# A mixture-of-experts stage whose first weights are half doubled by ScalarE and asked for at another point

## The chip, the cores and the metric

The kernel runs on one core of a Trainium2 chip. The metric is the device time of one execution in microseconds; lower is better. TensorE is called PE here, VectorE DVE, ScalarE ACT, GpSimd POOL and SyncE SP, as in the profile. SP does no arithmetic in this kernel, it waits for semaphores and issues DMA transfers.

## What is computed

The reference is a two-layer language-model tower over 64 x 128 tokens of width 192. In short:

```python
h = layernorm(tok_w[x] + pos_w + type_w[mask]) * gamma + beta
h = h + attention(layernorm(h))                       # layer 0
h = h + moe(layernorm(h))                             # the stage of this case
h = h + attention_with_relative_positions(layernorm(h))   # layer 1
h = h + fast_feed_forward(layernorm(h))

def moe(xf):                     # E = 8 experts, top K = 2, D = 192, I = 768
    gates = softmax(xf @ Wr + br)
    top_g, top_i = top_k(gates, 2)
    for e in range(8):
        w_e = sum(top_g * (top_i == e), axis=-1)
        y = gelu(xf @ W1[e] + b1[e], exact) @ W2[e] + b2[e]
        out = out + w_e[:, None] * y
```

## The kernel before

The kernel is one program in stages: layer 0 (64 token tiles in a software pipeline), the routing (which token goes to which seat of which expert), the expert stage, layer 1 and a short last stage. Only the expert stage is touched.

**Tiles of the expert stage.** The 16,384 pairs of token and expert are sorted by expert into 71 tiles (NBLK) of 256 rows (BLK), each tile with one expert. For each tile the kernel loads that expert's weights anew, gathers the tile's 256 token rows from `zn_d`, computes the 768 hidden values (transposed, in 6 chunks of 128, kept in `prob`, in the code `hT`), and the 192 outputs, and stores them to `ys_d`. All buffers of the stage are double: tile t uses number t mod 2.

**The product in parts.** Each fp32 weight w is split into a high part of the type float32r and a low part w - high, and so is x. DVE makes `w1hi` (L1152, two casts of 768 columns, one for rows 0 to 127 of the weights and one for rows 128 to 191) and `w1lo` (L1154, L1155, two subtractions). The weights have 192 rows; the second piece of them, 64 rows, was loaded twice, to partitions 0 to 63 and 64 to 127 of `w1[b][1]`. The rows gathered from `zn_d` hold the last 64 columns twice as well, so that on the second piece the upper 64 partitions of `xhi` can hold the low part of x (L1160): one product covers high and low. PE runs 5 products for each of 6 chunks (L1024 to L1030).

**The engines' programs**, all built by `pipeline` (L107), which calls a body for each step n and tells it by an age which tile each part works on: `load` has age 0, `h` age 1, `y` age 2.

- SP (`expert_sync`, L1172): at step n waits until all GELUs of tile n-2 are done (`h_sb`, L1194), issues the four loads of first weights and bias of tile n (L1199), waits until the outputs of tile n-2 are added (`y_sb`, L1201), issues second weights and their bias (L1203, L1205), and then stores the outputs of tile n-2 (L1210). It also issues, at step 2, the store of the routing table, at step 5 its reload (L1183), and at steps 4 to 7 four reads of `hres` for layer 1 (L1188), one a step, ahead of that step's loads.
- POOL (`expert_pool`, L947): gathers the rows of a tile (L964) when the tile of two before has been transposed.
- PE (`expert_tensor`, L983): transposes of tile t (L993, L994), second product of tile t-1 (L1005, called y here), waits for `xhi`, `xlo` and `split` of tile t, first product of tile t (L1030, called h).
- ACT (`expert_scalar`, L1050): copies the transposed x out of PSUM (`xhi`, L1055), then six GELUs (L1061), two behind each pair of chunks.
- DVE (`expert_vector`, L1144): waits for the first weights (L1150), splits them, makes `xlo` (L1158) and the low rows (L1160), and adds the output bias of tile t-1 (L1168, `ys`).

The first weights lie in the tile `score` by the profile's names, the second ones in `probT`, the output bias in `tok`.

Of the kernel before, what the change touches and what calls it, by code (L numbers as in the profile page):

```python
# [7 lines left out]
F32 = mybir.dt.float32  # L8
# [4 lines left out]
ACT = mybir.ActivationFunctionType  # L13
# [4 lines left out]
D1 = D - 128  # L18
# [5 lines left out]
E, TOPK, I = 8, 2, 768  # L24
NI = I // 128
BLK = 256
NBLK = T * B * TOPK // BLK + E - 1
# [42 lines left out]
def upto(t, tiles=NT):  # L70

    return max(0, min(t + 1, tiles)) if isinstance(t, int) else t + 1


def after(eng, sem, value):

    if not isinstance(value, int) or value > 0:
        eng.wait_ge(sem, value)
# [58 lines left out]
def settle(eng, spare):  # L137

    eng.sem_inc(spare, 1)


def tower(nc, ids_h, typ_h, tok_w, pos_w, type_w, gamma, beta,
# [7 lines left out]
    with ExitStack() as ctx:  # L150
# [6 lines left out]
        def sem(name):  # L157
            return ctx.enter_context(nc.semaphore(name))
# [64 lines left out]
        idx = two("idx", [128, 1], U32)  # L223
# [40 lines left out]
        b1s = two("b1s", [128, NI])  # L264
# [39 lines left out]
        spare = sem("spare")  # L304
# [598 lines left out]
                                         "tables", "lane", "seat", "seat_mm", "seated", "rows")}  # L903
        route_st, route_ld = sem("route_st"), sem("route_ld")
        h1_ld = [sem(f"h1_ld{c}") for c in range(4)]
        D_ = {n: sem("D_" + n) for n in ("xT_ps", "xhi_sb", "xlo_sb", "split", "dve", "idx", "h_ps", "h_sb", "y_ps", "y_sb")}
        w1_ld = [sem(f"w1_ld{p}") for p in range(2)]
        x_ld = [sem(f"x_ld{p}") for p in range(2)]
        w2_ld = [sem(f"w2_ld{p}") for p in range(2)]
        y_st = [sem(f"y_st{p}") for p in range(2)]  # L910
        ages_d = dict(load=0, h=1, y=2)
        NH = NI // 2
        ps_y = [ps_v, ps_k]

# [67 lines left out]

        def expert_tensor(pe):  # L983
            def body(st):
                t = st.n - 1
                if st.has("h"):
                    b = st.two("h")
                    pe.wait_ge(x_ld[b], 32 * (st.pair("h") + 1))

                    after(pe, D_["xhi_sb"], upto(t - 1, NBLK))  # L990
                    after(pe, D_["xlo_sb"], upto(t - 1, NBLK))
                    for s in range(2):
                        pe.transpose(ps_t[:, s * 128:s * 128 + 128], xs[b][:, s, 0:128], ident[:])  # L993
                        last = pe.transpose(ps_t[:, BLK + s * 128:BLK + s * 128 + 128], xs[b][:, s, 128:XW],  # L994
                                            ident[:])
                    last.then_inc(D_["xT_ps"], 1)
                if st.has("y"):
                    b = st.two("y")
                    pe.wait_ge(w2_ld[b], 32 * (st.pair("y") + 1))
                    after(pe, D_["y_sb"], upto(t - 2, NBLK))  # L1000
                    for j in range(NH):
                        pe.wait_ge(D_["h_sb"], NH * st.tile("y") + j + 1)
                        for c in (2 * j, 2 * j + 1):
                            for s in range(2):
                                last = pe.matmul(ps_y[s][:, 0:D], hT[b][:, c, s * 128:s * 128 + 128],  # L1005
                                                 w2[b][:, c, :], start=(c == 0), stop=(c == NI - 1))
                    last.then_inc(D_["y_ps"], 1)
                if st.has("h"):
                    b = st.two("h")
                    pe.wait_ge(D_["xhi_sb"], upto(t, NBLK))  # L1010
                    pe.wait_ge(D_["xlo_sb"], upto(t, NBLK))
                    pe.wait_ge(D_["split"], upto(t, NBLK))
                    for j in range(NH):

                        if not (isinstance(t, int) and t == 0):
                            pe.wait_ge(D_["h_sb"], NH * (t - 1) + j + 1)
                        for c in (2 * j, 2 * j + 1):
                            dst = ps_s[:, j, (c % 2) * BLK:(c % 2) * BLK + BLK]
                            u = slice(c * 128, c * 128 + 128)

                            terms = [(w1hi[b][0][:, u], xhi[b][:, 0:BLK]),  # L1024
                                     (w1lo[b][0][:, u], xhi[b][:, 0:BLK]),
                                     (w1hi[b][0][:, u], xlo[b][:]),
                                     (w1hi[b][1][:, u], xhi[b][:, BLK:2 * BLK]),
                                     (w1lo[b][1][:, u], xhi[b][:, BLK:2 * BLK])]
                            for k, (w, x) in enumerate(terms):
                                last = pe.matmul(dst, w, x, start=(k == 0), stop=(k == len(terms) - 1))  # L1030
                        last.then_inc(D_["h_ps"], 1)
            pipeline(pe, ages_d, body, tiles=NBLK)
# [17 lines left out]
        def expert_scalar(act):  # L1050
            def body(st):
                if st.has("h"):
                    t, b = st.tile("h"), st.two("h")
                    act.wait_ge(D_["xT_ps"], upto(t, NBLK))
                    act.activation(xhi[b][:], ps_t[:], ACT.Copy).then_inc(D_["xhi_sb"], 1)  # L1055
                    for j in range(NH):
                        act.wait_ge(D_["h_ps"], NH * t + j + 1)

                        after(act, D_["y_ps"], upto(t - 2, NBLK))
                        for c in (2 * j, 2 * j + 1):  # L1060
                            last = act.activation(hT[b][:, c, :], ps_s[:, j, (c % 2) * BLK:(c % 2) * BLK + BLK],  # L1061
                                                  ACT.Gelu, bias=b1s[b][:, c:c + 1])
                        last.then_inc(D_["h_sb"], 1)
            pipeline(act, ages_d, body, tiles=NBLK)
# [78 lines left out]

        def expert_vector(dve):  # L1144
            ch = Chain(dve, D_["dve"])

            def body(st):
                if st.has("h"):
                    t, b = st.tile("h"), st.two("h")
                    dve.wait_ge(w1_ld[b], 64 * (st.pair("h") + 1))  # L1150
                    for c in range(2):
                        ch.step(dve.tensor_copy(w1hi[b][c][:], w1[b][c]))  # L1152
                    ch.done()
                    dve.tensor_tensor(w1lo[b][0][:], w1[b][0], w1hi[b][0][:].bitcast(F32), ALU.subtract)  # L1154
                    dve.tensor_tensor(w1lo[b][1][:], w1[b][1], w1hi[b][1][:].bitcast(F32),  # L1155
                                      ALU.subtract).then_inc(D_["split"], 1)
                    dve.wait_ge(D_["xhi_sb"], upto(t, NBLK))
                    dve.tensor_tensor(xlo[b][:], ps_t[:, 0:BLK], xhi[b][:, 0:BLK].bitcast(F32), ALU.subtract)  # L1158
                    rest = xhi[b][D1:128, BLK:2 * BLK]
                    dve.tensor_tensor(rest, ps_t[D1:128, BLK:2 * BLK], rest.bitcast(F32), ALU.subtract)\  # L1160
                        .then_inc(D_["xlo_sb"], 1)
                if st.has("y"):
                    t, b = st.tile("y"), st.two("y")
                    dve.wait_ge(D_["y_ps"], upto(t, NBLK))

                    after(dve, y_st[b], 16 * st.pair("y"))
                    for s in range(2):
                        ins = dve.tensor_tensor(ys[b][:, s, :], ps_y[s][:, 0:D], b2s[b], ALU.add)  # L1168
                    ins.then_inc(D_["y_sb"], 1)
            pipeline(dve, ages_d, body, ch, 2, tiles=NBLK)  # L1170

        def expert_sync(sp):  # L1172
# [1 line left out]
            hv = h1_d.rearrange("(t b) d -> b t d", b=B)  # L1174

            def body(st):
                before2 = upto(st.n - 2, NBLK)
                if isinstance(st.n, int) and st.n == 2:
                    sp.wait_ge(B_["turned"], 1)
                    sp.dma_start(route_d.rearrange("q (n k) -> n q k", n=NT), turned[:]).then_inc(route_st, 16)  # L1180
# [9 lines left out]
                if st.has("load"):  # L1190
                    t, b = st.tile("load"), st.two("load")
                    ex = sp.value_load(etabi[0:1, bass.ds(t, 1)], min_val=0, max_val=E - 1)

                    after(sp, D_["h_sb"], NH * before2)  # L1194
                    settle(sp, spare)
                    loads = [(w1[b][0], w1h[bass.ds(ex, 1), 0:128, :]), (b1s[b][:], b1h[bass.ds(ex, 1)])]
                    loads += [(w1[b][1][r:r + D1, :], w1h[bass.ds(ex, 1), 128:, :]) for r in (0, D1)]
                    for dst, src in loads:
                        sp.dma_start(dst, src.rearrange("o k i -> (o k) i")).then_inc(w1_ld[b], 16)  # L1199

                    after(sp, D_["y_sb"], before2)  # L1201
                    settle(sp, spare)
                    sp.dma_start(probT[b][:, 0:NI * D], w2h[bass.ds(ex, 1), :, :].rearrange("o k i -> (o k) i"))\  # L1203
                        .then_inc(w2_ld[b], 16)
                    sp.dma_start(b2s[b], b2h[bass.ds(ex, 1), :].to_broadcast([128, D])).then_inc(w2_ld[b], 16)  # L1205
# [413 lines left out]
```

## Time and profile before

| | us |
|---|---|
| median of 3 runs | 1827.81 |
| lowest, highest | 1826.41, 1836.93 |
| the profiled execution | 1831.29 |
| its span, first to last instruction | 1829.6 |
| mean granted clock of TensorE over the span | 0.970 |

| engine | busy us | share of the span |
|---|---|---|
| PE | 1645.3 | 90% |
| DVE | 1314.9 | 72% |
| ACT | 1172.6 | 64% |
| POOL | 659.8 | 36% |

The times are from separate executions, the profile from one. Its page lists busy time per engine over the whole span, which is a mean over stages with different limits. The timeline lists instructions by start with their length, and in square brackets how long the engine sat idle before and what ended that. Names stand as output<-inputs, with buffer numbers left out. `SPq` is SP's queue of DMA issues: a length there is the time that the issue took, not the transfer.

### The profile page before, as it was taken

To read this page: it belongs to the slowest core of one execution; us is meant where nothing else is said; L and a number is where in the kernel's file an instruction comes from. 1 tells how busy PE (TensorE), PEld (TensorE's weight loads), DVE (VectorE), ACT (ScalarE), POOL (GpSimd) and SP (SyncE) were. 2 spreads that over 40 slices of the span, in tenths; PEclk is the share of its full clock that TensorE was granted. 3 is DMA by queue.
4 is the path that set the end of the run, shared out by engine and by line. 5 is a ranking of instruction groups with operands and counts; after the bars stand their busy time and mean duration, and the time that the engine had idled before them with its cause. 6 is when DMAs were issued, how large, how long until landed. Compare 5 with 4: busy or idle time off the path is not lost. (4 is left out here: it accounts for less than half of the span.)

```text
span 1829.6 us, 60456 instructions
## 1 busy us (share of the span) xinstructions
PE 1645.3 (90%) x19438; PEld 1502.9 (82%) x19438; DVE 1314.9 (72%) x2962; ACT 1172.6 (64%) x3337; POOL 659.8 (36%) x1326
## 2 busy tenths in 40 slices
PE   2999999999578799999999999579999999999966
PEld 2888888888367699999999999468888888888852
DVE  5888888887585255555555554289999999999855
ACT  2888888888374233333333333389999999999930
POOL 4455555553103133333333332334444444444200
PEclk9999999999788899999999999899999999999978
DMA  4122222222124978888888888377777777777614
GB/s 114 45 65 61 65 61 62 63 61 53 35 65 116 296 231 242 246 243 247 243 246 240 246 244 226 93 217 206 207 208 217 207 214 213 208 209 212 195 41 138
DMA packets 349282, 301.77 MB, mean 165 GB/s; under 512 B 43915, under 2 KB 314335, under 8 KB 349215
## 3 DMA queue, kind: packets, MB, share of 16 engines
q1 hardware_dynamic: 328878, 261.16, 49.6%
q0 software_dynamic: 16032, 37.51, 8.5%
q10 hardware_dynamic: 4304, 2.23, 0.5%
q8 instruction: 39, 0.64, 0.1%
q14 instruction: 29, 0.23, 0.0%
HBM read 207.77 MB, written 93.05 MB: 164 GB/s over the span
## 5 line engine op out<-in xcount | busy, mean ns | idle before, releaser
L1061 ACT ACTIVATE prob<-ps_s,b1s 128x256 f32<-128x256 f32 x426 | 179.2, 472 | 371.3 <-PE ps_s L1030 371.3
L1030 PE MATMUL ps_s<-xhi,w1hi_c 128*128 128x256 f32 x852 | 237.9, 297 | 19.8 <-DVE xhi L1160 18.1
L1030 PE MATMUL ps_s<-xhi,w1lo_c 128*128 128x256 f32 x852 | 228.5, 286 | 0.0
L964 POOL DMA_INDIRECT xs<-zn_d,idx x71 | 93.9, 1323 | 356.5 <-PE ps_t L994 354.0
L1152 DVE CAST w1hi_c<-score 128x768 fp32r<-128x768 f32 x142 | 73.3, 558 | 205.1 <-DMA score<-w1h 204.9
L1005 PE MATMUL ps_v<-probT,prob 128*128 128x192 f32 x852 | 208.3, 326 | 0.0
L1005 PE MATMUL ps_k<-probT,prob 128*128 128x192 f32 x852 | 208.1, 326 | 0.0
L396 PE MATMUL ps_q<-xT,wqk_c 128*128 128x128 f32 x1536 | 196.8, 279 | 1.1 <-ACT kT L643 0.6
L396 PEld LDWEIGHTS ps_q<-xT,wqk_c 128*128 128x128 f32 x1536 | 189.5, 196 | 1.9 <-ACT xT L664 1.0
L1030 PEld LDWEIGHTS ps_s<-xhi,w1hi_c 128*128 128x128 f32 x852 | 165.7, 195 | 22.4 <-issue 20.3
L1030 PEld LDWEIGHTS ps_s<-xhi,w1lo_c 128*128 128x128 f32 x852 | 165.8, 195 | 0.0
L583 ACT ACTIVATE prob<-score 128x768 f32<-128x768 f32 (+1 forms) x128 | 149.2, 1166 | 3.1
L1005 PEld LDWEIGHTS ps_k<-probT,prob 128*128 128x128 f32 x852 | 150.2, 190 | 0.0
L1005 PEld LDWEIGHTS ps_v<-probT,prob 128*128 128x128 f32 x852 | 146.6, 190 | 0.0
L735 DVE TENSOR_TENSOR score<-ps_s,relb 128x1536 f32<-128x1536 f32 x64 | 112.4, 1756 | 31.8 <-DMA relb<-rel_d 25.1
L456 PEld LDWEIGHTS ps_v<-vv,probT 128*64 128x64 f32 x3072 | 102.4, 139 | 30.6 <-issue 28.3
L1030 PE MATMUL ps_s<-xlo,w1hi_c 128*128 128x256 f32 x426 | 121.6, 285 | 0.0
L382 PE MATMUL ps_s<-kT,qT 32*64 32x64 f32 (+1 forms) x4608 | 113.4, 253 | 5.2 <-ACT xT L664 4.9
L456 PE MATMUL ps_v<-vv,probT 128*64 128x17 f32 x3072 | 113.3, 212 | 5.2 <-DVE hres L778 3.5
L382 PEld LDWEIGHTS ps_s<-kT,qT 32*64 32x64 f32 (+1 forms) x4608 | 91.9, 151 | 27.7 <-issue 27.5
L435 PE MATMUL ps_k<-ident,prob 128*128 128x128 f32 x704 | 112.8, 279 | 1.6 <-ACT prob L583 1.6
L321 POOL TENSOR_TENSOR rs<-veps,mhalf 128x1 f32<-128x1 f32 x192 | 108.1, 563 | 15.0
(217 smaller groups left out, 4385.1 us busy)
## 6 DMA issues: line engine op xcount, KB each, us to landing
rel_d<-rpad SPq DMA_DIRECT2D x64, 864.0 KB
relb<-rel_d SPq DMA_DIRECT2D x64, 768.0 KB, 4.7
probT<-w2h SPq DMA_DIRECT2D x71, 576.0 KB
score<-w1h SPq DMA_DIRECT2D x71, 384.0 KB
score<-w1h SPq DMA_DIRECT2D x142, 192.0 KB
ys_d<-ys SPq DMA_DIRECT2D x71, 192.0 KB
tok<-b2h SPq DMA_DIRECT2D x71, 96.0 KB
posb<-pos_w SPq DMA_DIRECT2D x128, 48.0 KB
```

The source lines that it names most:

```text
L321: pool.tensor_tensor(out[b][:], veps[b][:], mhalf[:, 0:1], ALU.pow).then_inc(S[out_ok], 1)
L382: last = pe.matmul(ps_s[t, g, a * keys:a * keys + keys], qT[q4][q, a // 2, t], kT[q4][q, a, t], start=True, stop=True)
L396: last = pe.matmul(ps_q[:, o:o + 128], qk_w[l][chunk][:, o:o + 128], (xT0, xT1)[chunk][b][:], start=(chunk == 0), stop=(chunk == 1))
L435: last = pe.transpose(ps_pt[u % 2][:, k * 128:k * 128 + 128], prob[b][:, j * 128:j * 128 + 128], ident[:])
L456: last = pe.matmul(ps_v[64 * c:64 * c + 64, j * W:(j + 1) * W], probT[b][:, j * 128 + 64 * c:j * 128 + 64 * c + 64], vv[v][:, j * W:(j + 1 ...
L583: act.activation(prob[b][:, 0:H * keys].rearrange("p (g a k) -> p g a k", g=G, a=A), score[b][:, :, :, 0:keys], ACT.Exp, scale=SCALE).then ...
L735: dve.tensor_tensor(sc, psv, relb[b][:].rearrange("p (g a) k -> p g a k", g=G), ALU.add).then_inc(S["s_rd"], 1)
L964: pool.indirect_dma_start(xs[b][:, s, :], None, zn_d, bass.IndirectOffsetOnAxis(ap=ix[b][:], axis=0)).then_inc(x_ld[b], 16)
L1005: last = pe.matmul(ps_y[s][:, 0:D], hT[b][:, c, s * 128:s * 128 + 128], w2[b][:, c, :], start=(c == 0), stop=(c == NI - 1))
L1030: last = pe.matmul(dst, w, x, start=(k == 0), stop=(k == len(terms) - 1))
L1061: last = act.activation(hT[b][:, c, :], ps_s[:, j, (c % 2) * BLK:(c % 2) * BLK + BLK], ACT.Gelu, bias=b1s[b][:, c:c + 1])
L1152: ch.step(dve.tensor_copy(w1hi[b][c][:], w1[b][c]))
```

## The change

- SP issues one load of the second piece of the first weights (to partitions 0 to 63) where it issued two.
- DVE casts and subtracts only partitions 0 to 63 of the second piece. The upper rows of `w1lo[.][1]` are cleared once, ahead of the stage. Low part of w times low part of x on these rows, a term of second order, is thereby left out, as it is on the first piece.
- ACT copies partitions 0 to 63 of the loaded second piece to partitions 64 to 127 of `w1hi[.][1]` for each tile, between `xhi` and the GELUs, and counts `twice`. PE waits for `twice` as well ahead of the first product.
- The ages are now `w1` 0, `load` 1, `h` 2, `y` 3. At step n SP works in this order: wait for `h_sb` of tile n-3, load b1 of tile n-1; wait for `split` and `twice` of tile n-2, load first weights of tile n; wait for `y_sb` of tile n-3, load second weights and bias of tile n-1; store tile n-3. The step numbers of the routing table and of the `hres` reads are as they were.
- b1 has a semaphore of its own, and ACT waits for it ahead of the GELUs.

```diff
-        ages_d = dict(load=0, h=1, y=2)
+        b1_ld = [sem(f"b1_ld{p}") for p in range(2)]
+        ages_d = dict(w1=0, load=1, h=2, y=3)
...
                     pe.wait_ge(D_["split"], upto(t, NBLK))
+                    pe.wait_ge(D_["twice"], upto(t, NBLK))
...
                     act.activation(xhi[b][:], ps_t[:], ACT.Copy).then_inc(D_["xhi_sb"], 1)
+                    act.wait_ge(w1_ld[b], 32 * (st.pair("h") + 1))
+                    act.activation(w1hi[b][1][D1:128, :], w1[b][1][0:D1, :], ACT.Copy).then_inc(D_["twice"], 1)
+                    act.wait_ge(b1_ld[b], 16 * (st.pair("h") + 1))
...
             ch = Chain(dve, D_["dve"])
+            for p in range(2):
+                ch.step(dve.memset(w1lo[p][1][D1:128, :].bitcast(F32), 0.0))
+            ch.done()
...
-                    dve.wait_ge(w1_ld[b], 64 * (st.pair("h") + 1))
-                    for c in range(2):
-                        ch.step(dve.tensor_copy(w1hi[b][c][:], w1[b][c]))
+                    dve.wait_ge(w1_ld[b], 32 * (st.pair("h") + 1))
+                    ch.step(dve.tensor_copy(w1hi[b][0][:], w1[b][0]))
+                    ch.step(dve.tensor_copy(w1hi[b][1][0:D1, :], w1[b][1][0:D1, :]))
...
-                    dve.tensor_tensor(w1lo[b][1][:], w1[b][1], w1hi[b][1][:].bitcast(F32),
+                    low = w1lo[b][1][0:D1, :]
+                    dve.tensor_tensor(low, w1[b][1][0:D1, :], w1hi[b][1][0:D1, :].bitcast(F32),
                                       ALU.subtract).then_inc(D_["split"], 1)
...
-                    after(sp, D_["h_sb"], NH * before2)
+                    after(sp, D_["h_sb"], NH * upto(t - 2, NBLK))
                     settle(sp, spare)
-                    loads = [(w1[b][0], w1h[bass.ds(ex, 1), 0:128, :]), (b1s[b][:], b1h[bass.ds(ex, 1)])]
-                    loads += [(w1[b][1][r:r + D1, :], w1h[bass.ds(ex, 1), 128:, :]) for r in (0, D1)]
+                    sp.dma_start(b1s[b][:], b1h[bass.ds(ex, 1)].rearrange("o k i -> (o k) i")).then_inc(b1_ld[b], 16)
+                if st.has("w1"):
+                    t, b = st.tile("w1"), st.two("w1")
+                    ew = sp.value_load(etabi[0:1, bass.ds(t, 1)], min_val=0, max_val=E - 1)
+
+                    after(sp, D_["split"], upto(t - 2, NBLK))
+                    settle(sp, spare)
+
+                    after(sp, D_["twice"], upto(t - 2, NBLK))
+                    settle(sp, spare)
+                    loads = [(w1[b][0], w1h[bass.ds(ew, 1), 0:128, :])]
+                    loads += [(w1[b][1][0:D1, :], w1h[bass.ds(ew, 1), 128:, :])]
                     for dst, src in loads:
                         sp.dma_start(dst, src.rearrange("o k i -> (o k) i")).then_inc(w1_ld[b], 16)
-
-                    after(sp, D_["y_sb"], before2)
+                if st.has("load"):
+                    t, b = st.tile("load"), st.two("load")
+
+                    after(sp, D_["y_sb"], upto(t - 2, NBLK))
```

## Rows read from the trace of the kernel before

**Rows 1.** PE row of the page's 40 slices, 45.7 us each, busy tenths.

```profile
PE   2999999999578799999999999579999999999966
```

**Rows 2.** Windows: length, PE, PEld, DVE, ACT, POOL busy, PEclk, DMA share, GB/s.

```profile
575.00:595.68 20.68, 20.68 (x151) 20.68 (x150) 9.96 (x20) 6.65 (x16) 7.81 (x12) 1.00 0.81 230
595.68:646.54 50.86, 35.92 (x235) 34.86 (x234) 17.13 (x32) 12.03 (x28) 11.71 (x16) 0.90 0.99 283
700.00:800.00 100.00, 100.00 (x736) 100.00 (x734) 52.04 (x100) 37.81 (x88) 33.35 (x51) 1.00 0.87 246
```

**Rows 3.** Timeline of ACT: start, length, line and operation, idle time before.

```profile
595.68 0.84 ACT L1061 ACTIVATE prob<-ps_s,b1s 128x256 f32<-128x256 f32 x2 [4.20 <-PE ps_s L1030]
...
646.54 0.84 ACT L1061 ACTIVATE prob<-ps_s,b1s 128x256 f32<-128x256 f32 x2 [6.37 <-PE ps_s L1030]
...
853.40 0.84 ACT L1061 ACTIVATE prob<-ps_s,b1s 128x256 f32<-128x256 f32 x2 [4.20 <-PE ps_s L1030]
...
861.33 0.84 ACT L1061 ACTIVATE prob<-ps_s,b1s 128x256 f32<-128x256 f32 x2 [4.20 <-PE ps_s L1030]
```

**Rows 4.** Timeline of ACT near the end of the expert stage.

```profile
1115.38 0.84 ACT L1061 ACTIVATE prob<-ps_s,b1s 128x256 f32<-128x256 f32 x2 [4.20 <-PE ps_s L1030]
...
1142.17 0.84 ACT L1061 ACTIVATE prob<-ps_s,b1s 128x256 f32<-128x256 f32 x2 [5.88 <-PE ps_s L1030]
```

**Rows 5.** Timeline of DVE between 600 and 645 us.

```profile
606.28 1.03 DVE L1152 CAST w1hi_c<-score 128x768 fp32r<-128x768 f32 x2 [11.16 <-DMA score<-w1h]
...
641.24 1.03 DVE L1152 CAST w1hi_c<-score 128x768 fp32r<-128x768 f32 x2 [7.20 <-DMA score<-w1h]
```

**Rows 6.** Timeline of one steady tile, SP's queue, DVE, PE and ACT.

```profile
850.02 1.15 SPq L1199 DMA_DIRECT2D score<-w1h  x2
...
853.09 0.34 SPq L1203 DMA_DIRECT2D probT<-w2h  x1
...
855.22 1.03 DVE L1152 CAST w1hi_c<-score 128x768 fp32r<-128x768 f32 x2 [2.29 <-DMA score<-w1h]
...
855.60 0.27 PE L993 MATMUL ps_t<-ident,xs 128*128 128x128 f32 x1
...
856.04 0.49 PE L1005 MATMUL ps_v<-probT,prob 128*128 128x192 f32 x2
...
856.53 0.60 ACT L1055 ACTIVATE xhi<-ps_t 128x512 fp32r<-128x512 f32 x1
...
858.46 0.43 DVE L1160 TENSOR_TENSOR xhi<-ps_t,xhi 64x256 fp32r<-64x256 f32 x1
...
859.80 0.42 PE L1030 MATMUL ps_s<-xhi,w1hi_c 128*128 128x256 f32 x1
```

**Rows 7.** Timeline of SP's queue from 580 to 598 us.

```profile
580.40 0.42 SPq L1210 DMA_DIRECT2D ys_d<-ys  x1
...
588.79 0.46 SPq L1188 DMA_DIRECT2D hres<-h_d  x1
...
591.23 4.36 SPq L1199 DMA_DIRECT2D score<-w1h  x1
...
596.31 1.12 SPq L1199 DMA_DIRECT2D score<-w1h  x2
```

**Rows 8.** DMA issues of the page: KB each.

```profile
probT<-w2h SPq DMA_DIRECT2D x71, 576.0 KB
score<-w1h SPq DMA_DIRECT2D x71, 384.0 KB
score<-w1h SPq DMA_DIRECT2D x142, 192.0 KB
```

**Rows 9.** Lines by form, ACT: count, busy us, mean ns, idle before.

```profile
L576 ACT ACTIVATE probT<-ps_q 128x512 f32<-128x512 f32 x64 | 38.3, 598 | 5.0 <-PE ps_q L435 5.0
...
L576 ACT ACTIVATE probT<-ps_q 128x384 f32<-128x384 f32 x64 | 31.9, 498 | 0.0
```

**Rows 10.** Timeline of ACT at the start of the expert stage.

```profile
566.88 0.60 ACT L1055 ACTIVATE xhi<-ps_t 128x512 fp32r<-128x512 f32 x1 [6.89 <-PE ps_t L994]
```

More of the change, by code:

```diff
@@ L905, in tower @@
         h1_ld = [sem(f"h1_ld{c}") for c in range(4)]
-        D_ = {n: sem("D_" + n) for n in ("xT_ps", "xhi_sb", "xlo_sb", "split", "dve", "idx", "h_ps", "h_sb", "y_ps", "y_sb")}
+        D_ = {n: sem("D_" + n) for n in ("xT_ps", "xhi_sb", "xlo_sb", "split", "twice", "dve", "idx", "h_ps", "h_sb", "y_ps", "y_sb")}
         w1_ld = [sem(f"w1_ld{p}") for p in range(2)]
@@ L984, in body @@
             def body(st):
-                t = st.n - 1
+                t = st.tile("h")
                 if st.has("h"):
@@ L1176, in body @@
             def body(st):
-                before2 = upto(st.n - 2, NBLK)
                 if isinstance(st.n, int) and st.n == 2:
```

## The prediction

> **What bounds the kernel now.** I read the page's slices first [rows 1]. Counted from 0 they are 45.7 us each. Slices 1 to 9 are layer 0, 12 to 24 the expert stage (about 560 to 1157 us), the rest layer 1. The change touches only the expert stage, so the views after that are of this stage alone. In it PE stands at 9 tenths from slice 14 on, after an 8 and a 7 in slices 12 and 13. The windows [rows 2] give the same in numbers: from 700 to 800 us PE is busy for all 100.00 us at full clock with DMA at 0.87. From 595.68 to 646.54 us PE is busy for only 35.92 of 50.86 us, with DMA at 0.99 and 283 GB/s. So over most of the stage PE is the limit, without a gap, and in one stretch near its start the DMA engines are.
>
> The timeline gives one tile's beat [rows 3]: the first GELU of a tile starts at 853.40 and of the next at 861.33, a period of 7.93 us. It is the ruler for the stall. In the dip the first GELUs start at 595.68 and 646.54, four tiles apart: 50.86 us where 4 x 7.93 = 31.7 us would do, **19.2 us lost**. Near the end of the stage the same reading gives a little more [rows 4]: 1115.38 to 1142.17 is 26.79 us for three tiles, **3.0 us lost**. Between the two places PE has no gap to speak of. All that any change of loads can give back here is 19.2 + 3.0 = 22.2 us.
>
> Who ends these waits? In the dip DVE's cast of the first weights sits idle for 11.16 us until `score<-w1h` lands, and still 7.20 us three tiles on [rows 5]. In a steady tile [rows 6] one sees how narrow that path is. Call T the start of the tile's transposes (855.60). The last first-weights load of that tile was issued by 851.17 and the cast starts at 855.22; DVE's last low part ends at 858.89 (T+3.3); PE starts the first product at 859.80 (T+4.2). That leaves 0.9 us. So first weights 1 us late stall PE. Everything else that is loaded is far from late: the second weights of this tile are asked for at 853.09, and the products that use them start only one period after 856.04, at 864.0.
>
> What makes them late is the queue [rows 7]. Four reads of `hres`, 1536 KB each, are put on SP's queue, one per tile step, the first at 588.79; behind it the issue of the next first weights takes 4.36 us, where an undisturbed one takes 0.34 [rows 6], and SP, which works in order, issues nothing else meanwhile.
>
> **The change, part by part.** *One load of two is dropped.* The page's issues [rows 8] have 142 of 192 KB for 71 tiles: two per tile beside one of 384 KB. With second weights of 576 KB a tile moves 0.393 + 2 x 0.197 MB of first weights, 0.688 of second weights and their bias (128 x 192 numbers more), 0.262 of gathered rows, 0.197 stored (by the shapes in the code): 1.935 MB, and 1.739 after. At the 283 GB/s of the stretch that is 0.69 us of DMA time per tile. In the steady part it is worth nothing, since PE covers it. It costs PE's work nothing either: the same 30 products per tile run, the low part's upper rows being zero now.
>
> *ACT copies 64 x 768.* The trace of before has no such copy. From below: 384 elements 0.498 us, from above 2 x 0.598 us, twice the 512-element copy [rows 9]. On the line through the two rows 768 elements come to 0.80 us, which I take. ACT's order is xhi, copy, GELUs. xhi ends at 857.13 (T+1.5), so the copy ends at T+2.3 (2.0 from below, 2.7 from above), while PE comes to its wait at T+4.2 after the second products. ACT itself sits idle 4.20 us before each first GELU [rows 3]. Cost: nothing. If that cover were gone, 0.80 us x 71 = 57 us. DVE's four operations keep their lengths (the row count fell, not the 768 columns): 0. The two clears of w1lo, once, write the width of the casts, of which two take 1.03 us [rows 6]; they go in front of the first split at 560 us, and the first xhi is not written before 566.88 [rows 10]: 0. Two more values read and two more waits on SP: they lie in SP's idle time.
>
> *First weights are asked for earlier.* Before: when the last GELU of two tiles back is done; the second-piece issues start at 850.02 [rows 6], T(n-1)+2.4, with two issues of 0.34 to 0.5 us ahead of them, so that wait ends at about T(n-1)+1.3. After: when split and copy of tile n-2 are done, T(n-2)+2.3. That is 6.9 us sooner, so their reserve grows from 0.9 to about 7.8 us. In SP's queue the first weights of tile n now stand before the second weights of tile n-1, not of tile n. Behind the new waits on SP stand w2(n-1), b2 and the store of tile n-3; they wait for y_sb(n-3) at T(n-2)+5.4 anyway, 3.1 us later than the new wait ends, so nothing is held back. The bias b1 is asked for at T(n-2)+1.3 for a GELU at T(n-1)+5.7: 12 us. At the start, w2(1) now waits for the copy of tile 0 (566.88 + 0.60 + 0.80 = 568.3, [rows 10]) instead of going out with the first loads; it is wanted 13 us later, two tiles on: no stall. The `hres` reads hang on step numbers, and the step now carries tile n-3's store in front: the first goes out right after tile 0's store at 580.40 [rows 7] instead of at 588.79.
>
> *Where the stall goes.* With w1 7.8 us early, the second weights are next. Asked for at T+5.4 (855.60 - 7.93 + 5.4 = 853.1, as the row says) and wanted at 864.0, they have 10.9 us. Their own landing isn't shown; the last 0.39 MB of first weights took 4.05 us from issue [rows 6], so I take 5 and a reserve of 6 us (bounds: 2.4 us of pure transfer gives 8.5; a landing as long as that in the dip, issued by 597.43 and there at 606.28, 8.9 us [rows 5, 7], gives 2). Now the debt. Casts at 606.28 and 641.24 [rows 5] put a step with an `hres` chunk at 34.96 / 3 = 11.65 us; after it is 10.96 us. Above the 7.93 us beat that is 3.7 before and 3.0 after. Four steps and 0.5 us for reading the routing table back (0.13 MB) make 15.4 before and 12.6 after. Less the reserve of 0.9: 14.5 before, against 19.2 measured, so 4.7 us of it (restart at a lower clock, 0.90 in the stretch against 1.00; a queue that is not served evenly) escape this sum. After: 12.6 - 6 = 6.6, or 11.3 with the same extra. I take 9. **Gain 19.2 - 9 = 10.2 us, and the 3.0 us at the end, since 7.8 us of reserve cover them: 13.2 us.** Nothing is added. The profiled execution took 1831.29 us (span 1829.6 and 1.7 around it); 1831.3 - 13.2 = 1818.1. It is 3.5 us above the median of 1827.81, so the median goes to 1814.6, say 1815.
>
> A rule weighs the 0.69 us otherwise. The Trainium skill, "SBUF — State Buffer", section "Door 1: The DMA port swizzle", says that DMA speed depends on how many of the 16 ports the partitions reach, and that partitions 0 to 63 reach only 8. By it each of the two 64-row loads takes 0.197 MB at half of its 435 GB/s = 0.9 us, and the one that stays is as slow as ever; the sum would be 4 x 0.2 = 0.8 us better. No row here separates the two loads, so the mean rate stands.
>
> **Rivals.** *All stalls go.* If the second weights' reserve is 8.5 us and the extra 4.7 doesn't return, 4.1 us of the debt are left, and the chunks' earlier start can work them off in the 0.19 that the DMA engines have free in the 20.68 us up to 595.68 [rows 2], 3.9 us. Against it: 6.3 MB at 283 GB/s are 22 us of DMA time, and each tile leaves only 7.93 - 6.14 = 1.8 us free. Time: 1827.8 - 22.2 = 1805.6.
>
> *The second weights take the whole place.* With a reserve of 2 us: stall 12.6 - 2 + 4.7 = 15.3, gain 3.9 + 3.0 = 6.9, 1821. For it: the blocked issue of 4 to 6 us hits w2 as it hit w1. Against: w2 never made PE wait in the dip.
>
> *The change does nothing.* Then the `hres` bytes alone set the dip's length and only 4 x 0.69 = 2.8 us of transfer come off: 1825.
>
> *Slower.* One mechanism: the copy on ACT comes onto PE's path. It decides once it ends after T+4.2, that is from 2.7 us per copy on; at 3.5 us it would cost 0.8 x 71 = 57 us, 1814.6 + 57 = 1872. Against it: that is over three times what [rows 9] give.
>
> **How the numbers follow.** Forecast (gain 8 to 18) 0.62; all stalls go 0.13; second weights in the whole place (4 to 8) 0.15; nothing 0.07; slower 0.03. About 1% is what a measurement of this kernel can tell from no change, 18.3 us. Only the first rival and the outer edge of the forecast reach it: faster by over 1% 0.14, slower 0.03, within 1% 0.83. The likeliest is 1815. The range takes in all the gaining cases: 1806 to 1825.
>
> **What the profile after would show.** Per tile one `score<-w1h` of 384 and one of 192 KB; an ACT copy of 64 x 768 of about 0.8 us; the steady period still 7.93 us with DMA near 0.78 instead of 0.87; no idle DVE cast before w1 in the steady part, with the cast right behind `ys`; first GELUs over the same four to six tiles late by 9 us in all, with PE waiting for `probT<-w2h` or its first y product; no loss at 1115 to 1142. It would be wrong if the steady period changed, if PE waited for ACT's copy, or if w1 were still what ends the dip.

## The result, and the profile after

| | before | after |
|---|---|---|
| median us, 12 runs each | 1832.16 | 1813.78 |
| lowest, highest | 1826.41, 1838.23 | 1810.72, 1822.04 |
| the profiled execution, its span | 1831.29, 1829.6 | 1812.49, 1810.7 |

The ratio is 0.991 (95% interval 0.9891 to 0.9929), just under 1% faster; the medians lie 18.4 us apart. The forecast was 1815 with 1806 to 1825. In a later comparison the changed kernel came to 0.991 again (0.9886 to 0.9934).

The page's slices after. To be set beside [rows 1]: PE busy and the DMA engines' share. PE is at 9 tenths from slice 14 on as before, but slice 13 has risen from 7 to 8 tenths, and the DMA share in the stage is at 7 where it was at 8.

```profile
PE   2999999999568899999999999489999999999966
...
DMA  4122222221113977777778778377777777777614
```

The windows after, columns as in [rows 2]. The stretch between the first GELUs of tiles 3 and 7 now takes 38.89 us instead of 50.86; the clock in it is 1.00 instead of 0.90. In the steady part the DMA engines' share fell from 0.87 to 0.72 for 11% fewer GB/s (over 700 to 1100 us from 0.86 to 0.74, for 10% fewer).

```profile
575.00:595.36 20.36, 20.36 (x149) 20.36 (x149) 10.54 (x22) 8.79 (x19) 6.65 (x12) 1.00 0.86 256
595.36:634.25 38.89, 32.44 (x234) 31.74 (x233) 16.74 (x33) 14.83 (x32) 10.78 (x16) 1.00 1.05 322
700.00:800.00 100.00, 100.00 (x731) 100.00 (x730) 52.07 (x100) 48.33 (x100) 28.84 (x52) 1.00 0.72 218
```

ACT's timeline after, beside [rows 3]. From 595.36 to 634.25 four tiles should take 31.7 us; 7.2 us are lost where 19.2 were. Three tiles in between have their GELUs held up by the bias `b1s`, a wait that the kernel before did not have.

```profile
595.36 0.84 ACT L1066 ACTIVATE prob<-ps_s,b1s 128x256 f32<-128x256 f32 x2 [3.38 <-issue]
...
604.26 2.30 ACT L1066 ACTIVATE prob<-ps_s,b1s 128x256 f32<-128x256 f32 x6 [4.36 <-DMA b1s<-b1h]
...
614.39 2.30 ACT L1066 ACTIVATE prob<-ps_s,b1s 128x256 f32<-128x256 f32 x6 [6.49 <-DMA b1s<-b1h]
...
624.65 2.42 ACT L1066 ACTIVATE prob<-ps_s,b1s 128x256 f32<-128x256 f32 x6 [6.60 <-DMA b1s<-b1h]
...
634.25 0.84 ACT L1066 ACTIVATE prob<-ps_s,b1s 128x256 f32<-128x256 f32 x2 [5.83 <-PE ps_s L1032]
```

PE's idle times in the dip, first of the kernel before, then after. Before, PE waits four times for the first weights: 7.66 + 1.50 + 3.91 + 1.86 = 14.9 us. After, it waits three times, and for something else: the bias of the second weights, `tok<-b2h`, which SP issues right behind the second weights: 2.02 + 2.20 + 2.24 = 6.5 us. The third group shows DVE in the changed kernel: in the same three tiles the first weights were late too, if less than the second ones.

```profile
610.05 0.55 PE L1030 MATMUL ps_s<-xhi,w1hi_c 128*128 128x256 f32 x1 [7.66 <-DVE xhi L1160]
...
621.40 0.36 PE L1030 MATMUL ps_s<-xhi,w1hi_c 128*128 128x256 f32 x1 [1.50 <-DVE xhi L1160]
...
633.49 0.36 PE L1030 MATMUL ps_s<-xhi,w1hi_c 128*128 128x256 f32 x1 [3.91 <-DVE xhi L1160]
...
645.00 0.36 PE L1030 MATMUL ps_s<-xhi,w1hi_c 128*128 128x256 f32 x1 [1.86 <-DVE xhi L1160]
```

```profile
608.05 0.59 PE L1006 MATMUL ps_v<-probT,prob 128*128 128x192 f32 x2 [2.02 <-DMA tok<-b2h]
...
618.44 0.59 PE L1006 MATMUL ps_v<-probT,prob 128*128 128x192 f32 x2 [2.20 <-DMA tok<-b2h]
...
628.87 0.59 PE L1006 MATMUL ps_v<-probT,prob 128*128 128x192 f32 x2 [2.24 <-DMA tok<-b2h]
```

```profile
606.08 0.56 DVE L1159 CAST w1hi_c<-score 128x768 fp32r<-128x768 f32 x1 [3.41 <-DMA score<-w1h]
...
616.74 0.56 DVE L1159 CAST w1hi_c<-score 128x768 fp32r<-128x768 f32 x1 [3.86 <-DMA score<-w1h]
...
626.84 0.56 DVE L1159 CAST w1hi_c<-score 128x768 fp32r<-128x768 f32 x1 [3.48 <-DMA score<-w1h]
```

A steady tile after, beside [rows 6]. T is 850.47. ACT's new copy runs from 852.02 to 852.86 (T+2.4) in the shadow of the second products, PE starts the first product at 854.68 (T+4.2) as before, DVE casts the next tile's weights at 855.65, right behind `ys` and without waiting for a load.

```profile
850.47 0.27 PE L994 MATMUL ps_t<-ident,xs 128*128 128x128 f32 x1
...
851.40 0.60 ACT L1057 ACTIVATE xhi<-ps_t 128x512 fp32r<-128x512 f32 x1
...
852.02 0.84 ACT L1059 ACTIVATE w1hi_c<-score 64x768 fp32r<-64x768 f32 x1
...
853.89 1.02 SPq L1217 DMA_DIRECT2D score<-w1h  x2
...
854.68 0.42 PE L1032 MATMUL ps_s<-xhi,w1hi_c 128*128 128x256 f32 x1
...
855.65 0.55 DVE L1159 CAST w1hi_c<-score 128x768 fp32r<-128x768 f32 x1
...
855.97 0.33 SPq L1223 DMA_DIRECT2D probT<-w2h  x1
```

At the end of the stage [rows 4] the loss is gone: six tiles take 47.61 us here, 7.93 each.

```profile
1086.07 0.84 ACT L1066 ACTIVATE prob<-ps_s,b1s 128x256 f32<-128x256 f32 x2 [3.34 <-PE ps_s L1032]
...
1133.68 0.84 ACT L1066 ACTIVATE prob<-ps_s,b1s 128x256 f32<-128x256 f32 x2 [3.39 <-issue]
```

**One ruler for all kernels.** GELUs are held up by b1 in some of the kernels below, so I read the beat off DVE instead: from the `ys` of one tile to that of the next. Over the first eight such steps, less eight beats (7.927 us each, with one more digit), the kernel before loses 19.2 us and the changed one 7.3; this is called the dip loss below. Over all 70 steps of the stage it is 22.9 and 6.8, so 16.1 of the 18.9 us between the two spans lie in the stage; 0.4 lie ahead of it and 2.4 behind it, where nothing was changed.

### The profile page after: what moved, and what is told of

Same layout as the page of the kernel before. It is cut to its first block and busy times, and to the rows that moved or that the text cites. A ratio compares the mean times of both kernels' runs of the same rounds, so it can differ in the third digit from the quotient of the medians.

```text
span 1810.7 us, 60890 instructions
## 1 busy us (share of the span) xinstructions
PE 1645.4 (91%) x19438; PEld 1504.3 (83%) x19438; DVE 1314.6 (73%) x2964; ACT 1231.2 (68%) x3408; POOL 629.9 (35%) x1326
## 5 line engine op out<-in xcount | busy, mean ns | idle before, releaser
L965 POOL DMA_INDIRECT xs<-zn_d,idx x71 | 69.4, 978 | 370.3 <-PE ps_t L995 367.8
L1177 DVE TENSOR_TENSOR ys<-ps_v,tok 128x192 f32<-128x192 f32 x71 | 25.4, 358 | 160.3 <-PE ps_k L1006 160.3
```

What stands on the lines that cost most here:

```text
L965: pool.indirect_dma_start(xs[b][:, s, :], None, zn_d, bass.IndirectOffsetOnAxis(ap=ix[b][:], axis=0)).then_inc(x_ld[b], 16)
```

## The experiments

**The load alone.** The kernel before with one load dropped and ACT's copy; weights asked for at the old place.

```diff
-                    loads += [(w1[b][1][r:r + D1, :], w1h[bass.ds(ex, 1), 128:, :]) for r in (0, D1)]
+                    loads += [(w1[b][1][r:r + D1, :], w1h[bass.ds(ex, 1), 128:, :]) for r in (0,)]
...
+                    act.activation(w1hi[b][1][D1:128, :], w1[b][1][0:D1, :], ACT.Copy).then_inc(D_["twice"], 1)
```

> The kernel before with only the single load and ACT's copy; the first weights are still asked for after the last GELU of two tiles back, the order on SP's queue is the old one. Theory (the earlier ask carries the gain, since first weights have 0.9 us of reserve and the bytes only take 0.69 us off each tile): the dip loses 12.6 - 0.9 + 4.7 = 16.4 us instead of 19.2, so 2.8 us faster than before, up to 4 with the end of the stage; DVE's cast still waits for score<-w1h in the dip. Rival (the dropped transfer carries the gain): 10 us or more faster, and the dip's loss near 8 us.

Ratio 0.993 (0.9898 to 0.9962). Dip loss 12.9 us, so 6.2 less than before, over twice what I expected; it lies between my 16.4 and the rival's 8. For the whole the rival was nearer: it wanted 10 us or more, the medians lie 10.8 apart, the ratio makes 12.8, and over the 70 steps this kernel is 10.5 us shorter than before, where I had 4 at most. PE's waits are 4.24 + 1.49 + 2.33 + 2.42 = 10.5 us and are still ended by the first weights (DVE's `xhi` comes behind the cast). The windows: the dip, and 700 to 1100 us, where the DMA share is 0.75 against 0.86 of the kernel before over the same 400 us.

```profile
611.52 0.55 PE L1031 MATMUL ps_s<-xhi,w1hi_c 128*128 128x256 f32 x1 [4.24 <-DVE xhi L1167]
...
622.56 0.36 PE L1031 MATMUL ps_s<-xhi,w1hi_c 128*128 128x256 f32 x1 [1.49 <-DVE xhi L1167]
...
633.06 0.36 PE L1031 MATMUL ps_s<-xhi,w1hi_c 128*128 128x256 f32 x1 [2.33 <-DVE xhi L1167]
...
643.65 0.36 PE L1031 MATMUL ps_s<-xhi,w1hi_c 128*128 128x256 f32 x1 [2.42 <-DVE xhi L1167]
```

```profile
595.00:650.00 55.00, 44.52 (x309) 43.46 (x308) 23.65 (x44) 21.39 (x44) 14.13 (x22) 0.97 0.97 284
700.00:1100.00 400.00, 400.00 (x2932) 399.93 (x2932) 214.63 (x404) 194.58 (x406) 119.11 (x200) 1.00 0.75 219
```

A second profile:

> The kernel load_only once more for a second profile: is its dip of 12.9 us reproducible? Theory: 11 to 15 us, ended by DVE's cast that waits for score<-w1h. Rival (chance): above 16 us, as my own sum had it.

It lost 12.5 us, with 9.9 us of waits, and is 11.0 us shorter than before over the stage. The number stands.

**The earlier ask alone.** The changed kernel with the second piece loaded twice, no copy.

```diff
-                    loads += [(w1[b][1][0:D1, :], w1h[bass.ds(ew, 1), 128:, :])]
+                    loads += [(w1[b][1][r:r + D1, :], w1h[bass.ds(ew, 1), 128:, :]) for r in (0, D1)]
```

> The changed kernel with the second piece loaded twice again and no copy on ACT: only the earlier ask and the new order remain. Theory: the dip loses about 10 us (a step with an hres chunk is 0.69 us longer than in the changed kernel, four of them on its 7.2), the 3.0 us at the end come back: 9.2 + 3.0 = 12 us faster than before, about 3 us slower than the changed kernel; PE waits for the second weights' bias tok<-b2h in the dip and DVE's cast is no longer the last. Rival (the dropped transfer carries the gain): within 4 us of before.

Ratio 0.9965 (0.9935 to 0.9994), dip loss 17.0 us: 2.2 us less than before where I expected 9.2. The whole is 6.4 us faster by the ratio, where I had 12 and the rival at most 4. The releaser is as expected, `tok<-b2h`, and the sum of the waits is 0.82 + 3.83 + 1.99 + 4.62 = 11.3 us.

```profile
600.48 0.59 PE L1006 MATMUL ps_v<-probT,prob 128*128 128x192 f32 x2 [0.82 <-DMA tok<-b2h]
...
612.51 1.01 PE L1006 MATMUL ps_v<-probT,prob 128*128 128x192 f32 x2 [3.83 <-DMA tok<-b2h]
...
625.57 0.59 PE L1006 MATMUL ps_v<-probT,prob 128*128 128x192 f32 x2 [1.99 <-DMA tok<-b2h]
...
638.37 0.59 PE L1006 MATMUL ps_v<-probT,prob 128*128 128x192 f32 x2 [4.62 <-DMA tok<-b2h]
```

```profile
595.00:650.00 55.00, 43.74 (x282) 42.80 (x282) 21.22 (x40) 14.59 (x35) 12.59 (x18) 0.91 1.00 281
700.00:1100.00 400.00, 400.00 (x2933) 400.00 (x2932) 215.49 (x406) 152.28 (x355) 111.36 (x200) 1.00 0.83 245
```

> The kernel ask_only once more for a second profile: is its dip of 17.0 us reproducible? Theory: 14 to 19 us, with at least one wait of PE above 3 us and a first y product of about 1.0 us behind it. Rival (chance): below 12 us.

The second profile lost 13.6 us, just under the 14 to 19 expected, with waits of 2.76 + 3.33 + 1.68 + 2.94 = 10.7 us and no first product as long as the 1.01 us above. So the loss varies by 3.4 us from one execution to the next, the waits by 0.6 only. At the end of the stage both single parts have nothing left of the loss; each of them alone is enough for it.

This run changes more than the ask. With the new order the first read of `hres` also goes out 2.3 us behind the first `ys` (582.15 us here, 580.56 in the changed kernel), where it was 10.2 us in the kernel before. No run separates the two, so what is called the earlier ask here is both together.

**Bytes, or the shape of the load?** The removed load cost more than its bytes. So, in the kernel of the earlier ask, the two loads of 64 rows became one of 128 rows. Partitions 0 to 63 then hold other rows of the weights than the product needs; only the time counts here.

```diff
-                    loads += [(w1[b][1][r:r + D1, :], w1h[bass.ds(ew, 1), 128:, :]) for r in (0, D1)]
+                    loads += [(w1[b][1][:, :], w1h[bass.ds(ew, 1), 64:, :])]
```

> The kernel ask_only (new order, two loads of 64 rows per tile) with these two loads made one load of 128 rows of the same 0.39 MB in all. It reads rows 64 to 191 of the weights, so partitions 0 to 63 hold the wrong rows; only the time is of interest. By the T-to-T ruler ask_only loses 17.0 us in the dip and the changed kernel 7.3. Theory P (a load that reaches 64 partitions is slow, the port rule, and a separate load has a price): one load of 128 rows costs about as little as one of 64, the dip loses about 9 us, DMA share in the steady part falls from 0.83 to about 0.75. Theory B (the bytes are the price): dip about 17 us, share 0.83, time as ask_only.

At the same 245 GB/s in the steady part the DMA share is 0.77 instead of 0.83 (0.84 in the second profile), and the dip loses 8.4 us instead of 17.0 and 13.6; PE's waits sum to 6.0 us. Nearly all that the dropped load gave in the dip comes back with every byte still moved. Ratio 0.9941 (0.9914 to 0.9969).

```profile
613.12 1.01 PE L1006 MATMUL ps_v<-probT,prob 128*128 128x192 f32 x2 [3.84 <-DMA tok<-b2h]
...
623.73 0.59 PE L1006 MATMUL ps_v<-probT,prob 128*128 128x192 f32 x2 [0.86 <-DMA tok<-b2h]
...
633.22 0.59 PE L1006 MATMUL ps_v<-probT,prob 128*128 128x192 f32 x2 [1.29 <-DMA tok<-b2h]
```

```profile
700.00:1100.00 400.00, 400.00 (x2931) 400.00 (x2931) 214.98 (x406) 151.82 (x354) 111.68 (x202) 1.00 0.77 245
```

So two loads of 64 rows are dearer than one of 128 rows of the same size: 0.06 x 7.93 us = 0.5 us of all the engines' time per tile. Whether it is the 64 partitions or the second transfer by itself that costs, this run doesn't separate.

By the Trainium skill, "SBUF — State Buffer", section "Door 1: The DMA port swizzle", a load of 64 partitions reaches half of the ports. The direction of the 0.83 against 0.77 agrees with it; the size is known from this run alone.

**Is the late bias b1 the new limit?** Four buffers for b1, asked for with the first weights.

```diff
-        b1s = two("b1s", [128, NI])
+        b1s = four("b1s", [128, NI])
...
+                    sp.dma_start(b1s[st.four("w1")][:], b1h[bass.ds(ew, 1)].rearrange("o k i -> (o k) i"))\
+                        .then_inc(w1_ld[b], 16)
```

> The changed kernel with four buffers for the bias b1, asked for right behind the first weights of its tile and two steps earlier in tiles than before, so that no load of b1 stands behind an hres chunk ahead of its GELUs. Theory (the second weights and their bias are what PE waits for in the dip, b1 lies in their shadow): the ACT waits for b1s<-b1h of 4.4, 6.5 and 6.6 us go, but PE still waits about 2 us before each of three y products, the dip loses 6 to 7.3 us, the whole is within 1.5 us of the changed kernel. Rival (the late bias is the dip's new limit): the dip falls to 3 us or less, 4 us faster than the changed kernel.

ACT's waits for b1 are gone, PE's waits are not: 2.33 + 0.97 + 3.02 = 6.3 us against 6.5, again for `tok<-b2h`. b1 lay in the shadow of the second weights. The loss as a whole was 12.0 us, not the 6 to 7.3 expected, with the clock in the dip at 0.91 instead of 1.00; ratio 0.9963 (0.9937 to 0.9988). That is a miss of the expectation (within 1.5 us of the changed kernel) in the part that isn't waiting (see the table below), and it isn't the profile's alone: the interval doesn't reach the 0.9891 to 0.9929 of the changed kernel, though the two were measured on different chips. The profile shows where part of its own 5.6 us lies: in the 4 us behind the wait of 3.02 us PE ran 14 products at a clock of 0.50, while the changed kernel ran 34 at 1.00 in the same window. Why the clock fell here and not there stays open.

```profile
608.40 0.59 PE L1006 MATMUL ps_v<-probT,prob 128*128 128x192 f32 x2 [2.33 <-DMA tok<-b2h]
...
619.25 0.59 PE L1006 MATMUL ps_v<-probT,prob 128*128 128x192 f32 x2 [0.97 <-DMA tok<-b2h]
...
630.46 1.00 PE L1006 MATMUL ps_v<-probT,prob 128*128 128x192 f32 x2 [3.02 <-DMA tok<-b2h]
```

```profile
632.00:636.00 4.00, 4.00 (x14) 4.00 (x13) 0.00 (x0) 0.00 (x0) 0.00 (x0) 0.50 0.80 259
```

**How wide is the cover of ACT's copy?** Four copies in a row.

```diff
+                    for again in range(1, 4):
+                        act.wait_ge(D_["twice"], 4 * t + again)
+                        act.activation(w1hi[b][1][D1:128, :], w1[b][1][0:D1, :], ACT.Copy).then_inc(D_["twice"], 1)
```

> The changed kernel with ACT's copy made four times in a row, each waiting for the one before. One copy takes 0.84 us and ends at T+2.5; PE comes to its wait at T+4.2, so about 1.8 us of it lie free. Four copies end at T+1.5 + 4 x 0.9 = T+5.1. Theory: the period of a tile grows by 0.9 us from 7.93 to about 8.8, 64 us more in all, and PE's idle time before the first product is ended by ACT w1hi. Rival (ACT's own line becomes the limit in another place, the GELUs): period above 9.3 us. If the copy had no cover at all, the period would grow by 3 x 0.9 = 2.7 us.

The beat grew from 7.93 to 8.76 us, 1868.3 us in all (one run; before beside it 1826.34). Over the 70 steps it is 56 us more than in the changed kernel, where 64 were expected; in the first eight steps only 3.6 came on top. Three more copies of 0.87 us are 2.6 us, of which about 0.8 showed: 1.8 us per tile lay free. PE's weight loads and products now wait for the copy, by 0.9 and 0.6 us at most (view of the waits, 700 to 1100 us: total, times, longest).

```profile
PEld ps_s L1032 <- ACT w1hi_c L1062: 38.7, 45, 0.9
...
PE ps_s L1032 <- ACT w1hi_c L1062: 25.4, 45, 0.6
```

**Out of the way.** The four reads of `hres` moved to the start of SP's program, behind the first two tiles' loads, while the routing runs.

```diff
                 if isinstance(st.n, int) and st.n == 2:
+                    for c in range(4):
+                        sp.dma_start(hres[:, 16 * c:16 * c + 16, :], hv[:, 16 * c:16 * c + 16, :])\
+                            .then_inc(h1_ld[c], 16)
                     sp.wait_ge(B_["turned"], 1)
```

> The changed kernel with the four reads of hres put on SP's queue right behind the loads of the first two steps, while the routing runs and the DMA engines are nearly idle. Theory (the dip is these reads and nothing else): no loss between the GELUs of tiles 3 and 7, the 7.2 us that the changed kernel still loses there come back, ratio to before 0.991 - 0.004 = 0.987. Rival (another cause, such as the lateness of the bias b1, holds part of the dip): 3 us or more stay. Second rival: the reads delay the gathered rows of the first tile, which then start PE later by some us.

> The kernel before with the four reads of hres put on SP's queue right behind the loads of the first two steps. Theory: the dip of 19.2 us goes wholly, the 3.0 us at the end stay: about 19 us faster than before, ratio 0.990, and only about 3 us slower than the changed kernel with the same move. Then the change itself is worth only those 3 us once the reads are out of the way. Rival (first weights with 0.9 us of reserve are late now and then in other places too): 12 us or less gained.

Both dips vanished: 0.1 us in the changed kernel, 0.5 in the old one. Ratios 0.9886 (0.9823 to 0.9949) and 0.9899 (0.9846 to 0.9952). In the old kernel 4.4 us stay over the whole stage, the changed one loses none. So once the reads are out of the way, the change itself is worth some 5 us in the stage, and the two ratios, of four runs each, don't tell the kernels apart. The second rival isn't borne out: PE waits 5.86 us for the first tile's rows in the changed kernel with the early reads and 5.80 without, 6.41 and 6.36 in the old one. To settle the rest:

> The changed kernel with the hres reads during the routing once more, with more rounds, beside the changed kernel on the same chip. Theory: no dip, 7.3 us less than the changed kernel, ratio to before 0.986 to 0.988. Rival (the reads disturb the routing or layer 1): the ratio is not below that of the changed kernel.

> The changed kernel once more, for a second profile of the dip and a second interval. Theory (a wait of PE near 2 us costs only itself, one above 3 us also brings a stretch at the lower clock): the dip's loss is 7 to 9 us again, with three waits of PE near 2 us before y's first product and a granted clock of 1.00 in the stretch. Rival (the 7.3 us were luck of one execution): 10 us or more. Ratio to before 0.990 to 0.993.

On one chip the changed kernel came to 1813.39 us, 0.991 (0.9886 to 0.9934), and the one with the early reads to **1802.67 us, 0.9859 (0.9831 to 0.9886)**. It beats both kernels, by about 26 us against before and 11 against the change, of which the dip's 7.8 us are shown. The second profile of the changed kernel lost 7.8 us in the dip with 5.3 us of waits; its clock in the stretch was 0.97, not the 1.00 I had written, with 0.65 from 608 to 612 us, right behind the longest wait of 2.56 us. The last windows are of the early reads: DMA stands at 0.75, 1.09 and 0.90 from 520 to 550 us, where the kernel before has 0.79, 0.00 and 0.00 (its middle window stands last), and PE is busy for all 55.00 us of what had been the dip.

```profile
520.00:530.00 10.00, 9.59 (x57) 8.74 (x55) 8.03 (x28) 9.37 (x28) 0.00 (x0) 0.83 0.75 216
530.00:540.00 10.00, 9.24 (x60) 7.76 (x60) 8.49 (x31) 9.71 (x32) 0.00 (x0) 1.00 1.09 330
540.00:550.00 10.00, 9.33 (x62) 8.01 (x61) 8.31 (x30) 9.63 (x31) 0.00 (x0) 1.00 0.90 266
595.00:650.00 55.00, 55.00 (x405) 55.00 (x404) 29.32 (x56) 26.68 (x56) 15.29 (x28) 1.00 0.75 223
```

```profile
530.00:540.00 10.00, 9.38 (x62) 8.06 (x61) 8.42 (x31) 9.62 (x31) 0.00 (x0) 1.00 0.00 0
```

## Why the prediction was right, and where its steps were not

The forecast of 1815 against 1813.78 is closer than its working, and that is luck. The gain of 13.2 us was 5.2 short of the 18.4 between the medians. The starting point, 1827.81 from three runs, was 4.4 under the 1832.16 of twelve. The two errors nearly cancel. Two more cancel in part within the gain, the price of the dropped load and the worth of the earlier ask (below).

The dip by its parts, one row per profile (DVE ruler; waits are PE's idle times in it, summed; clock from 595 to 650 us):

| kernel | loss | PE's waits | rest | clock |
|---|---|---|---|---|
| before | 19.2 | 14.9 | 4.2 | 0.91 |
| ask alone | 17.0, 13.6 | 11.3, 10.7 | 5.7, 2.9 | 0.91, 0.97 |
| load alone | 12.9, 12.5 | 10.5, 9.9 | 2.4, 2.6 | 0.97, 0.97 |
| after | 7.3, 7.8 | 6.5, 5.3 | 0.9, 2.6 | 1.00, 0.97 |
| ask, one load of 128 rows | 8.4 | 6.0 | 2.4 | 0.97 |
| b1 early | 12.0 | 6.3 | 5.6 | 0.91 |

- **What bounds the stage** held: the beat stayed at 7.93 us, little but the dip and the stage's end gave anything (one more wait of 0.61 us behind the dip, at 669.63), and without the `hres` reads there is no dip. The 22.2 us I took as the ceiling were 22.9.
- **The debt sum** held for what it summed, the waits, in the kernel before: 14.5 us worked out, 14.9 measured. The 6.6 for the kernel after, against 6.5 and 5.3, was reached by two wrong terms.
- **The 4.7 us that escaped the sum** are the rest column: the time by which PE was busy longer than its eight beats, its products behind a wait running at the lower clock. It goes with the granted clock (4.2 to 5.7 at 0.91, 2.4 to 2.9 at 0.97, 0.9 at 1.00) and not with the kernel. I had let half of it return (9 between 6.6 and 11.3); 0.9 and 2.6 did. So the dip gave 11.8 us where I had 10.2, and the rest of the stage 4.3 (16.1 - 11.8) where I had 3.0 from three tiles at its end; that is why 13.2 us were short of the 16.1 that the stage gave.
- **The two parts were weighed wrongly.** My sum gave the dropped load 4 x 0.69 = 2.8 us of waits and the earlier ask 6 - 0.9 = 5.1. By the runs the load alone took off 4.4 and 5.0, the ask alone 3.7 and 4.2, both 8.5 and 9.7; they add up. Over all 70 steps the load alone took off 10.5 and 11.0, the ask alone 6.5 and 9.9, both 16.1 and 15.6. The step that failed is the price of the load, "at the 283 GB/s of the stretch that is 0.69 us". The DMA share in the steady part fell by 0.11 (before to load alone) or 0.09 (ask alone to after), which is 0.9 or 0.7 us per tile, and in the dip it was worth 1.1 to 1.3 (4.4 and 5.0 over four). The run with one load of 128 rows says what the price hangs on: with every byte still moved, the waits fell from 11.3 and 10.7 to 6.0. The two errors cancelled. The forecast of 0.78 for the steady share missed likewise: 0.72 to 0.74. The rule that I set beside the sum as worth 0.8 us more pointed the right way.
- **The earlier ask** moved the wait from the first to the second weights, as forecast, with `tok<-b2h` as the last to land. The reserve of 6 us for w2 was too large: with the debt of 15.4 us, the waits of 11.3 and 10.7 in the ask alone leave 4.1 and 4.7. Nor would all stalls have gone with the second weights out of the way. In the changed kernel DVE was done with the first weights 2.2, 1.9 and 2.2 us before PE's first product in the three tiles (ends at 609.73, 620.39, 630.50, products at 611.92, 622.31, 632.73), while PE had by then been held 2.0, 4.2 and 6.5 us by w2. Had they landed at the same times without those holds, PE would have waited about 4.2 us for the first weights, an estimate near the 12.6 - 7.8 = 4.8 that the prediction's own terms give.
- **The bias b1** I had called 12 us early. In the dip its own issue, right behind a read of `hres`, took 3.2 to 6.0 us, and it held up the GELUs of three tiles. It cost PE no wait, since the second weights were later still.
- **ACT's copy**: 0.84 us where I took 0.80, ended at T+2.4; 1.8 us of cover, shown by four copies. The slower rival had a real mechanism, and its edge lies about where I put it: the 2.6 us of extra copies put about 0.8 on the beat, so PE begins to wait when the copies take 2.6 us in all, where I had 2.7.
- **"The change does nothing"** fell with the DMA shares and the waits; **"second weights in the whole place"** fell since the waits halved.

Still open: why a dropped load is worth more in the congested queue (1.1 to 1.3 us a tile) than in the steady part (0.7 to 0.9), and what makes up the 3 us beyond the dip between the changed kernel and the one with early reads (1813.39 - 1802.67 - 7.8), a difference that the intervals may cover by themselves. Open too: how the earlier ask and the earlier `hres` reads share the second part, and why the kernel with the early bias came out slower than the changed one.

## What to carry to other kernels

A stall near a burst of large transfers is a debt: so much more per step than the beat, less the reserve of whatever is wanted first; work out the reserve of every load, since an earlier ask only hands the wait to the next one. Price a transfer by the shape as well as by its bytes, and read the price from the DMA share at equal GB/s. And before tuning what the burst hits, look in the slices for a stretch where the DMA engines stand idle, and move the burst there.

## What the runs showed of the hardware that I had not expected

- Two loads to 64 partitions cost more than one of the same bytes to 128: DMA share 0.83 against 0.77 at 245 GB/s both. The 0.83 came back as 0.84 in a second profile, the 0.77 is of one.
- The same kernel runs in two lengths about 10 us apart, and its profiles show where: the drain of layer 1, when its software pipeline runs empty. From the last score addition to the end it took 80.3 us in one profile of the changed kernel and 92.3 in the other, 80.9 and 89.8 in the two with early reads, 79.2 and 89.7 in the two of the load alone. The windows are of the changed kernel, first the shorter, then the longer: 178 products in 16.0 us at a clock of 0.92, and 174 in 23.6 us at 0.50. The runs of the kernel before fall into two groups as well (1826 to 1830 and 1834 to 1838), though no profile here shows its longer one. So a median of few runs is a mixture, and a difference in one stage is better read in that stage.

```profile
1741.00:1757.00 16.00, 12.21 (x178) 9.70 (x178) 5.69 (x22) 6.06 (x26) 2.95 (x8) 0.92 0.01 2
```

```profile
1741.00:1764.60 23.60, 20.83 (x174) 17.03 (x174) 5.95 (x21) 6.19 (x25) 2.97 (x8) 0.50 0.00 1
```

- The first gather issue of each pair on POOL fell from a median of 1.40 to 0.97 us (700 to 1100 us) with the earlier split on DVE (0.97 with the ask alone too, 1.10 with the load alone), and the share of the gathers' queue from 14.6% to 11.5%. It gave no time here, and its cause wasn't tried.
